# A three-block perceiver on one core: output projection by batch instead of by chunk, and one weight split moved to two other engines

## The reference, cut to what matters

```python
x = x + xattn(layernorm(x), ctx_1024)   # cross-attention over 2048 keys, softmax over the 16 heads
x = x + attn(layernorm(x))              # self-attention with relative positions, Eq/Ek/Ev tables
x = x + ffn(layernorm(x))               # third attention-like block with gates
# x is (4, 128, 512); every weight is 512 x 512. In the first block:
out = einsum('hbqk,bkhd->bqhd', attn, v).reshape(B, S, 512)
return out @ Wo + bo
# in the second: q, k, v = y @ Wq, y @ Wk, y @ Wv with y = layernorm(x)
```

## Time and profile before

| | us |
|---|---|
| median of 3 runs | 744.22 (742.63 to 744.83) |
| profiled execution, its own time | 745.07 |
| its span in the trace | 743.1 |
| TensorE busy | 716.2 (96%) |
| VectorE busy | 628.5 (85%) |
| ScalarE busy | 490.5 (66%) |
| GpSimd busy | 502.0 (68%) |

### The profile page before, as it was taken

How to read it: one execution, slowest core, us unless ns; L and a number is a source line. 1 busy time by engine, 2 the same in 40 slices (tenths; PEclk the granted TensorE clock), 3 DMA queues, 4 the chain that set the end, 5 groups by cost and what they waited for, 6 DMA issues and landing times.

```text
span 743.1 us, 17302 instructions
## 1 busy us (share of the span) xinstructions
PE 716.2 (96%) x7542; PEld 569.6 (77%) x7542; DVE 628.5 (85%) x514; ACT 490.5 (66%) x694; POOL 502.0 (68%) x282
## 2 busy tenths in 40 slices
PE   8999999999999999999999999999988999889988
PEld 7777777777787777877777787777766667767876
DVE  5479999999999999999999999999965468887685
ACT  5578577786776877777786776867724445635681
POOL 0165969899898988989889898997992020063300
PEclk9999999999999999999999999999999999999999
DMA  8310110101011010110101101010011799521101
GB/s 334 115 59 1 58 57 2 57 2 57 15 45 58 2 58 1 58 58 1 59 1 59 36 24 58 2 57 2 2 58 57 275 395 367 233 101 58 58 2 57
DMA packets 15339, 55.71 MB, mean 75 GB/s; under 512 B 1696, under 2 KB 2080, under 8 KB 11680
## 3 DMA queue, kind: packets, MB, share of 16 engines
q1 hardware_dynamic: 15264, 54.61, 20.2%
HBM read 43.13 MB, written 11.47 MB: 73 GB/s over the span
## 4 chain that ended last, share of the span: by engine, by line
PE 80%; DVE 12%; ACT 5%; issue 3%; POOL 0%; ACTq 0%; DVEq 0%; POOLq 0%
PE ps L389 25%; PE ps L370 24%; PE ps L478 9%; PE ps L505 7%; PE ps L378 2%; PE ps L626 2%; PE ps L427 2%; DVE blocks L1498 1%; PE ps L739 1%; ACT v_buf L921 1%; DVE extra L1392 1%; DVE extra L1421 1%; DVE ps L1421 1%; PE ps L529 1%; DVE s_buf L1414 1%
## 5 line engine op out<-in xcount | busy, mean ns | idle before, releaser
L1261 POOL TENSOR_TENSOR s_buf<-s_buf,r_all 128x1024 f32<-128x1024 f32 x93 | 197.2, 2162 | 3.6 <-DVE r_all L1434 3.6
L945 ACT ACTIVATE s_buf<-s_buf 128x1024 f32<-128x1024 f32 x128 | 135.7, 1065 | 9.9 <-DVE s_buf L1414 9.1
L929 ACT COPY s_buf<-ps 128x1024 f32<-128x1024 f32 x128 | 123.3, 1018 | 20.6 <-PE ps L478 20.6
L1392 DVE TENSOR_REDUCE extra<-s_buf 128x128 f32<-128x2048 f32 x48 | 109.5, 2281 | 10.5 <-ACT s_buf L929 10.5
L1414 DVE TENSOR_TENSOR s_buf<-s_buf,ps 128x2048 f32<-128x2048 f32 x48 | 106.9, 2283 | 0.5
L1239 POOL TENSOR_TENSOR w_lo<-raw,w_hi 128x2048 fp32r<-128x2048 f32 x6 | 27.5, 4590 | 95.6 <-ACT w_hi L896 95.6
L921 ACT COPY v_buf<-ps 128x512 f32<-128x512 f32 x64 | 37.6, 588 | 78.9 <-PE ps L389 59.4
L1228 POOL TENSOR_TENSOR v_buf<-v_buf,extra 128x512 f32<-128x512 f32 x64 | 81.2, 1313 | 9.4 <-ACT v_buf L921 9.4
L1421 DVE TENSOR_REDUCE ps<-s_buf 128x128 f32<-128x4096 f32 x16 | 70.8, 4428 | 17.5 <-ACT s_buf L945 17.5
L1234 POOL TENSOR_TENSOR odd_lo<-extra,odd_hi 128x512 fp32r<-128x512 f32 x32 | 41.1, 1310 | 54.8 <-ACT odd_hi L904 54.8
L478 PE MATMUL ps<-q_t,k_t 32*128 32x128 f32 x2048 | 75.1, 283 | 2.3 <-ACT v_buf L921 0.6
(11 more groups left out here) (221 smaller groups left out, 1449.9 us busy)
## 6 DMA issues: line engine op xcount, KB each, us to landing
rel_scratch<-blocks SPq DMA_DIRECT2D x16, 636.0 KB, 10.9
s_buf<-rel_scratch SPq DMA_DIRECT2D x7, 1210.0 KB, 10.0
raw<-in_ctxT SPq DMA_DIRECT2D x8, 1024.0 KB, 4.9
extra<-in_ctxT SPq DMA_DIRECT2D x8, 1024.0 KB, 4.9
raw<-in_Wq SPq DMA_DIRECT2D x2, 1024.0 KB, 6.5
raw<-in_Wv SPq DMA_DIRECT2D x2, 1024.0 KB, 4.8
extra<-in_EvRel SPq DMA_DIRECT2D x1, 2048.0 KB, 12.6
extra<-rel_scratch SPq DMA_DIRECT2D x1, 1210.0 KB, 10.2
```

The lines of the kernel that those rows point to most:

```text
L929: copy(piece(t, 2 * w + u).rearrange("p e (u n) -> p (e u) n", u=2), ps[:, 2 * u:2 * u + 2, :]).then_inc(s["s_evac"], 1)
L945: nc.scalar.activation(piece(t, p), piece(t, p), ACT.Exp).then_inc(s["exp_done"], 1)
L1261: pool.tensor_tensor(part, part, spread(r_all, 4), ALU.mult).then_inc(s["attn_pool"], 1)
L1392: nc.vector.tensor_reduce(m_ps if k == 0 else m_next[:, k % 2, :], over_pairs(t, 2 * k, 2), AX.XY, ALU.max).then_inc(s["max_done"], 1)
```

## The change

1. TensorE. `out_proj1(c)` is replaced by `out_first()` and `out_rest(b)`. `out_first` does, right behind `attend(T - 1, 0)`, the two terms of chunk 0 with the high part of the activations for batches 0, 2 and 3 (6 matmuls). `out_rest(b)` does all that is left of a batch before the next one: 10 matmuls for batches 0, 2 and 3, and 12 for batch 1. `residual_in(1)` moves behind `out_rest(0)`. The transposes stand together at the end, without `keep_warm`.
2. VectorE and ScalarE. VectorE finishes the normalisation of a batch before it turns to the next. ScalarE does square root and residual copy of batches 0 to 2 in turn, then the square root of batch 3, the four `split_hi`, and the last residual copy.
3. Wq2. The cast goes from ScalarE to GpSimd (`tensor_copy`). The subtraction is cut in two: GpSimd does chunks 0 and 1, VectorE chunks 2 and 3, behind its four `split_lo`, under a new semaphore `wq2_lo`. `queries2` and SyncE's load of Wv2 wait for both.

```diff
             def rel_store(n):
@@ SyncE, weight_load(n)
+                if n == 3:
+                    sp.wait_ge(s["wq2_lo"], 1)
                 load(weight_raw(n), a[WEIGHTS[n][0]], "wodd_in" if n == 1 else "wraw_in")
@@ TensorE
+            def out_term(b, c, u, v, last):
+                return mm(ps[:, OUT_BANKS[b], :], ctx_parts[1][u][:, c, b * P:(b + 1) * P], w_parts[v][:, 0, c, :],
+                          start=False, stop=last, skip_group_check=True)
+            FIRST_OUT = (0, 2, 3)
+            def out_first():
+                pe.wait_ge(s["x_hi_done"], C + 1)
+                pe.wait_ge(s["wo_lo"], 1)
+                for b in FIRST_OUT:
+                    for u, v in PARTS[:2]:
+                        out_term(b, 0, u, v, False)
+            def out_rest(b):
+                for c in range(C):
+                    if b == 0 and c > 0:
+                        pe.wait_ge(s["x_hi_done"], C + c + 1)
+                        pe.wait_ge(s["wo_lo"], c + 1)
+                    for u, v in PARTS[2:] if c == 0 and b in FIRST_OUT else PARTS:
+                        if b == 0 and u:
+                            pe.wait_ge(s["x_lo_done"], c + 1)
+                        last = out_term(b, c, u, v, c == C - 1 and u == 1)
+                last.then_inc(s["wo_psum"], 1)
...
-            for w in range(C):
-                if w == C - 1:
-                    residual_in(1)
+            attend(T - 1, 0)
+            out_first()
+            for w in range(1, C):
                 attend(T - 1, w)
-            for c in range(C):
-                out_proj1(c)
-            transposes(y_ln, 1, 0)
-            keep_warm(LN_BANKS[3], 3)
-            transposes(y_ln, 1, 1)
-            keep_warm(LN_BANKS[3], 3)
-            transposes(y_ln, 1, 2)
-            transposes(y_ln, 1, 3)
+            out_rest(0)
+            residual_in(1)
+            for b in range(1, B):
+                out_rest(b)
+            for b in range(B):
+                transposes(y_ln, 1, b)
@@ TensorE, queries2
                     weight_ready(2)
+                    pe.wait_ge(s["wq2_lo"], 1)
@@ ScalarE
-            ln_std(1, 0)
-            ln_std(1, 1)
-            weight_hi(2)
-            ln_std(1, 2)
-            split_hi(1, 0)
-            ln_std(1, 3)
-            split_hi(1, 1)
-            residual1(0)
-            split_hi(1, 2)
-            split_hi(1, 3)
-            for b in range(1, B):
+            for b in range(B - 1):
+                ln_std(1, b)
                 residual1(b)
+            ln_std(1, B - 1)
+            for b in range(B):
+                split_hi(1, b)
+            residual1(B - 1)
@@ GpSimd
-            for n in range(1, 4):
-                weight_lo(n)
+            weight_lo(1)
+            pool.wait_ge(s["wraw_in"], 16 * 2)
+            pool.wait_ge(s[WEIGHTS[2][1]], WEIGHTS[2][2])
+            pool.tensor_copy(w_hi[:, 0], raw[:]).then_inc(s["wsplit_hi"], 1)
+            pool.wait_ge(s["wsplit_hi"], 3)
+            pool.tensor_tensor(w_lo[:, 0, 0:2], raw[:, 0:2], w_hi[:, 0, 0:2], ALU.subtract).then_inc(s["wsplit_lo"], 1)
+            weight_lo(3)
@@ VectorE
-            moments1(0)
-            moments1(1)
-            normalised(1, 0)
-            moments1(2)
-            normalised(1, 1)
-            moments1(3)
-            normalised(1, 2)
-            normalised(1, 3)
+            for b in range(B):
+                moments1(b)
+                normalised(1, b)
             for b in range(B):
                 split_lo(1, b)
+            dve.wait_ge(s["wsplit_hi"], 3)
+            tt(w_lo[:, 0, 2:4], raw[:, 2:4], w_hi[:, 0, 2:4], ALU.subtract).then_inc(s["wq2_lo"], 1)
```

More of the change, by code:

```diff
@@ L230, in probs_t @@
             return blocks[:, u * B:(u + 1) * B]
-        names = """x_in wq_in wk_in wv_in cols_in bv_in bo_in tab_in ctx_in_0 ctx_in_1 ctx_hi ctx_lo wq_split xq_split wkv_hi wkv_lo wraw_in wodd_in wsplit_hi wsplit_lo wo_lo
+        names = """x_in wq_in wk_in wv_in cols_in bv_in bo_in tab_in ctx_in_0 ctx_in_1 ctx_hi ctx_lo wq_split xq_split wkv_hi wkv_lo wraw_in wodd_in wsplit_hi wsplit_lo wo_lo wq2_lo
             tab_mul ones_done pos_psum pos_done x_hi_done x_lo_done small_in
```

## The result

The changed kernel takes 741.09 us, the median of 18 runs (738.23 to 742.76), against 743.74 us for the kernel before (18 runs, 741.38 to 745.05). The ratio is 0.996, with a 95% interval of 0.9951 to 0.9968. Forecast were 741.6 us and a gain of 2.65 us; the medians differ by 2.65 us. The profiled execution took 739.54 us (span 737.3) and stands at the fast end of the 18.

What follows compares the result with a forecast made beforehand. TensorE, 80% of the chain, was taken as the bound. keys2 2.7 us earlier, less 0.05 for the tight fit, Wq2 costing 0, gave 2.65: 744.22 - 2.65 = 741.6 us, range 740.3 to 743.6.

Steps and rivals of the forecast that it cites:

- The valley: From the last projection matmul to keys2: 4.1 us instead of 6.77, keys2 starting 2.7 us earlier.
- 0.8 to 1.0 named as a sign: TensorE before the last transposes: one gap of 0.8 to 1.0 us would show the forecast right.
- The fit without slack: Normalisation: one batch's chain of 2.26 us just fits under the next batch's 2.29; 0.05 us taken off the gain.
- The first part: TensorE up to the projection's end: within 0.1 us of now; low clock elsewhere moves it by -0.4 to +0.2 us.
- The Wq2 split: Cast and halved subtraction before queries2: cast 2.6 us on GpSimd, all done at 569.7 to 570.0, before 570.3, cost 0.
- the two bounds: GpSimd's Wq2 cast: between 1.90 us, as ScalarE's, and 4.53, as GpSimd's own two-input operation.
- The rule on two SBUF inputs: VectorE's half would wait for GpSimd's: 0.25 us, harmless, with a 2.6 us cast; 1.7 us late with 4.53.
- The rival of the clock: Behind the projection, the granted clock falls in the new valley: price 1.4 to 1.6 us, time 743.1; chance 15%.
- The fall at 547: Granted clock 0.50 in 547 to 550, at the attend steps; out_first's six matmuls there take 2.6 us, 0.43 each.
- DMA rival: Stores and loads from 577 on, not TensorE, set the second block; gain doesn't reach the end, 743.5 to 744.2; 6%.

Runs made afterwards that it cites:

- run 7: The changed kernel with 11 more filler matmuls in TensorE's wait ahead of the last attend steps; 739.6 us, ratio 0.9938.
- run 8: The kernel before with 11 more filler matmuls in TensorE's wait ahead of the last attend steps; 741.44 us, ratio 0.997.
- run 6: The changed kernel without the six out_first matmuls, with 11 more fillers ahead of the last attend steps; 739.45 us, ratio 0.9951.
- run 9: The changed kernel with VectorE's half of the Wq2 subtraction moved ahead of its four split_lo, beside GpSimd's half; 744.24 us, ratio 1.0013.
- run 2: The changed kernel with the Wq2 cast back on ScalarE and the whole subtraction on GpSimd; 742.66 us, ratio 0.9993.
- run 3: The changed kernel with the whole Wq2 subtraction on GpSimd, besides the cast, and none on VectorE; 738.93 us, ratio 0.9943.
- run 5: The changed kernel without the six out_first matmuls, all twelve of a batch in its own turn; 740.98 us, ratio 0.9958.
- run 4: The kernel before with only the Wq2 part of the change; 744.03 us, ratio 1.0005.
- run 1: The changed kernel again, no edit; 740.26 us, ratio 0.9955. Its table sorts executions of changed and before by mean granted clock.
- clean pair: Changed kernel and kernel before, both with 11 fillers ahead of the last attend steps, granted clock 1.00 throughout; spans 736.1 and 739.4 us.

## Why the prediction was right, point by point

- **The valley.** `keys2` was to start 4.1 to 4.2 us behind the last projection matmul; it does so 4.16 us behind. The working (0.43 to the statistics, 2.26 for one batch, 1.43 to `keys2`) holds within 0.03 us in every part: 561.45 to 561.89, to 563.37 + 0.81 = 564.18, to 565.61. The wait before the last transposes was 1.07 us, a little above the 0.8 to 1.0 named as a sign.
- **The fit without slack.** The chain of a batch took 2.28 us against 2.26 for ten matmuls. VectorE went from batch 2 to batch 3 without a wait, and batch 3 was late by 0.01 to 0.02 us. The 0.05 us taken off was hardly needed.
- **The first part, a size that was off.** The sum gave the new order of the projection 0.06 us (563.36 to 563.30; the mean of the two values named there is 563.32), reckoned for a low clock. In the traces at full clock it is 0.62 us (runs 7 and 8): 0.36 between run 6 and run 7, which differ by the early terms, and the rest between run 8 and run 6, from the order behind them. With the low clock it is 18.37 - 18.12 = 0.25 us (run 9's trace has its last projection matmul at 561.75 and its first `attend` at 543.63). I allowed for an end up to 0.4 us earlier than the 0.09 reckoned; the value at full clock lies outside by 0.1.
- **The Wq2 split.** The cast took 1.89 us, the lower of the two bounds and not my 2.6. The split was done at 567.7, with `queries2` at 568.43: cost 0, as forecast. That the cast leaves ScalarE is needed (run 2); that VectorE helps is not (run 3). The prediction priced neither of the two by itself.
- **The rule on two SBUF inputs.** The sum did not hang on this rule of the Trainium skill, because VectorE's half began 0.14 us after GpSimd's had ended. Run 9 shows it at work. The cover was thinner than the prediction made it look: with the cast of 2.6 us that I took, GpSimd's half would have ended near 567.06, and VectorE's, free at 566.49, would have been done near 568.3, just ahead of the 568.43 of `queries2` (an estimate from these traces).
- **The rival of the clock.** In the profiled execution it did not come true; in run 5's it did, at the forecast price. The fall at 547 that the sum took as fixed is not fixed: it was there in the traces of before and of runs 2, 4, 5 and 9, and absent in those of the changed kernel, of runs 1 and 3, and of all with fillers.
- **The end of the program.** What `keys2` gained reached the end: 3.2 us in the interval, 3.3 in the spans of the clean pair. The first store of the relative terms started 572.35 - 565.61 = 6.74 us behind `keys2`, before 576.89 - 570.13 = 6.76: it moved with TensorE. The DMA rival falls.
- **The number.** That 2.65 us came out on the hundredth is luck: the interval of the ratio allows 2.4 to 3.6 us. The valley (2.62) is understood. The first part was underrated, by 0.2 us where the clock is low near 547 and by 0.6 where it is not: with the low clock there in both kernels the parts add up to 2.87 us, at full clock the times give 3.1. What brings the medians back to 2.65 is that most executions of both kernels have two low stretches, and two cost the changed kernel 2.9 us and the kernel before 2.5 (the table of run 1). At the place near 547 that is 1.5 against 1.13 us. Where the low stretches of the executions without a trace lay is not known, only how many there were.

## What to carry to other kernels

Before a barrier that needs all batches, order the last matrix product so that batches end apart by at least as long as one batch's chain takes: all but the last chain then lie under matmuls. The room that this makes is lost if any engine on the last chain has a long instruction queued there (1.9 us of cast took 1.4 back, a blocked subtraction nearly all of it), so such an edit and its neighbours in the queues are one change and are to be priced together. To see a gain of this size, compare executions at the same mean granted clock, and traces interval by interval, rather than medians or spans.

## What the runs showed of the hardware that I had not expected

- GpSimd's cast of 128 x 2048 from fp32 to the matmul format took 1.89 us, while its subtraction with two inputs takes 4.6 us on as many columns. In this cast, with one input, it is as fast as ScalarE (1.88 to 1.90).
- VectorE with two SBUF inputs stood still for 2.1 us beside a GpSimd subtraction (3.31 us instead of 1.21), and GpSimd was not slowed. The profile shows this as busy time of VectorE, not as a wait: an instruction on 20 columns stands there with 2.10 us instead of 0.17.
- The same kernel's executions differ by up to 4.5 us (738.23 to 742.76). Eleven fillers of 0.22 us in one wait took 2.5 us off the median of the kernel before, all of it by the clock. None of the four traces with them has the stretch at 0.50 near 547; of the eight without them, five have it.
